# A decoder block on one core: attention's output projection as three fp32r passes instead of one f32 pass

## The reference, cut to what matters

```
qh, kh, vh = split_heads(x @ Wq), split_heads(context @ Wk), split_heads(context @ Wv)   # 8 x 2048 x 128 each
sim  = einsum('hid,hjd->hij', qh, kh) * 128 ** -0.5
mean = sim.mean(-1);  sim = (sim - mean) * 1.5 + mean
attn = softmax(sim)
out  = einsum('hij,hjd->hid', attn, vh)            # per head 2048 x 128
x    = x + merge_heads(out) @ Wout + bout          # the output projection: per head 128 x 256 of Wout
```

## Time and profile before

| | us |
|---|---|
| median of 3 runs | 1335.17 |
| lowest and highest of them | 1331.78, 1336.15 |
| the profiled execution, device time | 1332.3 |
| its span in the profile | 1330.2 |
| PE busy | 1287.7 (97%) |
| DVE, ACT, POOL busy | 1023.5 (77%), 895.9 (67%), 907.9 (68%) |
| TensorE clock granted, mean | 0.99 |

### The profile page before, as it was taken

How to read it: one execution, slowest core, us unless ns; L and a number is a source line. 1 busy time by engine, 2 the same in 40 slices (tenths; PEclk the granted TensorE clock), 3 DMA queues, 4 the chain that set the end, 5 groups by cost and what they waited for, 6 DMA issues and landing times. The chain is left out here.

```text
span 1330.2 us, 22729 instructions
## 1 busy us (share of the span) xinstructions
PE 1287.7 (97%) x8358; PEld 1077.1 (81%) x8358; DVE 1023.5 (77%) x1628; ACT 895.9 (67%) x1315; POOL 907.9 (68%) x645
## 2 busy tenths in 40 slices
PE   5999999999999999999999999999999999988998
PEld 4688888888887788888888888888888888777998
DVE  6355498759317889999999999999999899985554
ACT  4555433425655878878778778778787777775774
POOL 2544410225410899989989999999999989863553
PEclk9999999999999999999999999999999999997999
DMA  6703032246764989988888888888888888796672
GB/s 219 104 6 74 4 101 81 67 130 245 208 233 140 247 213 231 221 196 216 215 203 215 216 201 218 215 196 221 214 201 217 201 191 208 185 252 244 203 230 76
DMA packets 172377, 241.35 MB, mean 181 GB/s; under 512 B 34179, under 2 KB 78085, under 8 KB 172272
## 3 DMA queue, kind: packets, MB, share of 16 engines
q1 hardware_dynamic: 155040, 208.11, 62.0%
q10 hardware_dynamic: 15184, 25.96, 5.7%
q0 software_dynamic: 2048, 5.90, 1.1%
HBM read 64.79 MB, written 41.32 MB: 80 GB/s over the span
## 5 line engine op out<-in xcount | busy, mean ns | idle before, releaser
L1217 POOL TENSOR_TENSOR xa_pT<-xa_moved,xa_pT 128x1024 fp32r<-128x1024 f32 x246 | 589.0, 2428 | 27.1 <-ACT xa_pT L1735 26.0
L1557 PE MATMUL xa_S<-xa_kT,xa_qT 128*128 128x512 f32 x1536 | 389.1, 401 | 1.2 <-ACT xa_probs L1741 1.2
L1741 ACT ACTIVATE xa_probs<-xa_S,xa_mx_nb_rinv 128x1024 f32<-128x1024 f32 x256 | 285.9, 1117 | 146.8 <-DVE xa_mx_nb_rinv L1339 146.8
L1574 PE MATMUL xa_O<-xa_pT,xa_v 128*128 128x512 f32 x1536 | 377.2, 394 | 2.9 <-DVE xa_pT L1392 2.6
L1336 DVE TENSOR_REDUCE xa_mx_nb_rinv<-xa_S 128x1 f32<-128x1024 f32 x256 | 305.3, 1211 | 78.1 <-PE xa_S L1557 78.0
L1574 PEld LDWEIGHTS xa_O<-xa_pT,xa_v 128*128 128x128 f32 x1536 | 289.0, 189 | 69.9 <-DVE xa_pT L1392 2.9
L1557 PEld LDWEIGHTS xa_S<-xa_kT,xa_qT 128*128 128x128 f32 x1536 | 288.5, 188 | 67.9 <-ACT xa_probs L1741 2.9
L1349 DVE STREAM_TRANSPOSE xa_tq<-xa_probs 128x1024 f32<-128x1024 f32 x256 | 316.7, 1238 | 15.0 <-ACT xa_probs L1741 7.3
L1735 ACT ACTIVATE xa_pT<-xa_moved 128x1024 fp32r<-128x1024 f32 x254 | 253.9, 1050 | 2.1 <-PE xa_O L1574 1.1
L506 PE MATMUL fw_pp<-fw_hT,fw_wqk 128*128 128x512 f32 x384 | 95.0, 405 | 4.3 <-DVE fw_hT L647 4.3
L506 PEld LDWEIGHTS fw_pp<-fw_hT,fw_wqk 128*128 128x128 f32 x384 | 73.4, 194 | 20.7 <-DVE fw_hT L647 3.0
(11 more groups left out here) (247 smaller groups left out, 1679.1 us busy)
## 6 DMA issues: line engine op xcount, KB each, us to landing
xa_moved<-xa_tq SPq DMA_DIRECT2D x508, 256.0 KB, 4.5
heads_k<-ci_outs SPq DMA_DIRECT2D x32, 256.0 KB, 2.0
heads_v<-ci_outs SPq DMA_DIRECT2D x32, 256.0 KB, 2.3
heads_q<-ci_outs SPq DMA_DIRECT2D x32, 256.0 KB, 2.4
xa_chunk<-heads_v ACTq DMA_DIRECT2D x32, 256.0 KB, 4.2
ex_w1s<-in_L_ffn_w_dram SPq DMA_DIRECT2D x8, 1024.0 KB, 7.3
ex_w2s<-in_L_ffn_w_dram SPq DMA_DIRECT2D x8, 1024.0 KB, 9.7
xa_chunk<-heads_q ACTq DMA_DIRECT2D x31, 256.0 KB, 4.2
```

The source lines that it names most:

```text
L1217: pool.tensor_tensor(quadrants(pT[LO], r), unit_moved(r), quadrants(pT[HI], r).bitcast(F32), ALU.subtract).then_inc(lo_ready, 1)
L1557: last = pe.matmul(banks[:, k % 2], qT[a][:, i // GT % 2, q], kT[b][h % 2][:, k * 512:(k + 1) * 512], start=(n == 0), stop=(n == 2))
L1574: last = pe.matmul(O[:], v[a][:, j * P:(j + 1) * P], pT[b][:, r % PRING, k], start=(j == 0 and n == 0), stop=(j == JT - 1 and n == 2))
L1741: act.activation(probs[:, unit % RING], S[:, score_banks(unit)].rearrange("p a b -> p (a b)"), ACT.Exp, bias=nb[:, s % 2:s % 2 + 1], scale ...
```

## The change

- For groups 0 to 27 (heads 0 to 6, `SPLIT_GROUPS = 28`) ACT copies the bank `O` into `oTs[HI]` as fp32r, at the end of slot 4g+10 and not at the start of slot 4g+11, and DVE subtracts it from `O` into `oTs[LO]` (`output_low`, first on DVE in slot 4g+11). The bank is free for `weighted` when that is done: PE waits for `out_lo`.
- The head of Wout is split too, as a thirteenth chunk ("w", h, 0) of each head from 0 to 6 in the table: HI part on ACT, LO part on POOL, 128 x 256.
- A projection of two tiles is then 6 fp32r matmuls (3 parts for each tile) in place of 2 float32 ones (4 instructions). Head 7 stays as it was.
- Projections and additions of groups 0 to 27 come one slot later (4g+12, 4g+14 and 4g+13, 4g+15).
- The ring `chunk` is gone: its place holds `oTs[HI]` and the two parts of Wout. A chunk lands in the buffer of its own LO part (`raw_k`, `raw_v`, `raw_q`), ACT writes its HI part, and POOL subtracts in place. The load is issued at the end of the slot before the one in which it is split, and takes over the waits for the old contents from `chunk_high`.
- The table of chunks is new: k, q, v and w in slots 0, 1, 3 to 8 and 10 to 14 of a head. SP loads `woh` at the start of each head, once the "w" chunk of the head before is split.

```diff
+        raw_k = [home(f"xa_rawk{i}", f"kT{i}", [P, TOK], F32, LO * 4 * TOK) for i in range(2)]
...
+        wohs = [home(f"xa_wouts{a}", "chunk", [P, D], F32R, 4 * (GCOLS + D * a)) for a in (HI, LO)]
...
+        oTs = [home("xa_oT_hi", "chunk", [P, GCOLS], F32R),
+               nc.alloc_sbuf_tensor_at("xa_oT_lo", [P, GCOLS], F32R, offset=oT_at)]
...
+        SPLIT_GROUPS = SLOTS // GT - 4
...
         def output_slot(g, k):
-            return SLOTS + OUTPUTS[g, k] if (g, k) in OUTPUTS else (g + 1) * GT + LAG + 2 * k
+            return SLOTS + OUTPUTS[g, k] if (g, k) in OUTPUTS else (g + 1) * GT + LAG + 2 * k + (g < SPLIT_GROUPS)
         def sum_slot(g, k):
-            return SLOTS + SUMS[g, k] if (g, k) in SUMS else (g + 1) * GT + LAG + 1 + 2 * k
+            return SLOTS + SUMS[g, k] if (g, k) in SUMS else (g + 1) * GT + LAG + 1 + 2 * k + (g < SPLIT_GROUPS)
+        def group_of_outputs(s):
+            g, phase = divmod(s - LAG - GT, GT)
+            return g if phase == 0 and 0 <= g < SPLIT_GROUPS else None
...
-            plan = {0: ("k", h + 1, 0), 1: ("q", h, 1), 2: ("k", h + 1, 1), 3: ("k", h + 1, 2), 4: ("v", h, 0),
...
+            plan = {0: ("k", h + 1, 0), 1: ("q", h, 1), 3: ("k", h + 1, 1), 4: ("q", h, 2), 5: ("v", h, 0), 6: ("v", h, 1),
...
+            def output_low(g):
+                dve.wait_ge(oT_ready, g + 1)
+                if g:
+                    dve.wait_ge(y_mm, 2 * g)
+                dve.tensor_tensor(by_tile(oTs[LO][:]), by_quadrant(O[:]), by_tile(oTs[HI][:]).bitcast(F32),
+                                  ALU.subtract).then_inc(out_lo, 1)
...
             for s in range(END):
+                g = group_of_outputs(s)
+                if g is not None:
+                    output_low(g)
                 if s < SLOTS:
                     maxima(s)
...
-                if q == 0 and g:
+                if q == 0 and 0 < g <= SPLIT_GROUPS:
+                    pe.wait_ge(out_lo, g)
+                elif q == 0 and g:
                     pe.wait_ge(oT_ready, g)
...
-                    last = pe.matmul(output_bank(g, k)[:, m], oT[:, t * P:(t + 1) * P], woh[:], start=True, stop=True)
+                    if g < SPLIT_GROUPS:
+                        for n, (a, b) in enumerate(PARTS):
+                            last = pe.matmul(output_bank(g, k)[:, m], oTs[a][:, t], wohs[b][:], start=(n == 0), stop=(n == 2))
...
-                if GT <= p <= SLOTS and p % GT == 0:
+                if GT <= p <= SLOTS and p % GT == 0 and group_of_outputs(s) is None:
                     copy_oT(p // GT - 1)
...
+                if group_of_outputs(s + 1) is not None:
+                    copy_oT(group_of_outputs(s + 1))
                 if s < SLOTS:
                     for c in chunks_of(s):
                         chunk_high(c)
+                    for c in chunks_of(s + 1) if s + 1 < SLOTS else ():
+                        if c[0] != "w":
+                            load(place[c])
```

More of the change, by code:

```diff
@@ L904, in cross_block @@
         first_in = [sem(f"xa_first_in{i}") for i in range(FIRST)]
-        chunk_in = [sem(f"xa_chunk_in{i}") for i in range(CRING)]
+        chunk_in = sem("xa_chunk_in")
         chunk_hi, chunk_lo = sem("xa_chunk_hi"), sem("xa_chunk_lo")
@@ L1063, in staged @@
                 return moved[:].rearrange("p r q j n -> p (r q j n)")[:, n * UNIT:(n + 1) * UNIT]
-            return chunk[:, n % CRING]
+            kind, h, part = order[n]
+            cols = slice(part * UNIT, (part + 1) * UNIT)
+            if kind == "k":
+                return raw_k[h % 2][:, cols]
+            if kind == "w":
+                return woh[:]
+            return raw_v[:, cols] if kind == "v" else raw_q[:, part % 2]
         def target(c, a):
@@ L1147, in _ @@
                 h, i = divmod(p, TILES)
[L1148 to L1149 removed]
+                if h and i == 0:
+                    sp.wait_ge(chunk_lo, place["w", h - 1, 0] + 1)
                     sp.dma_start(woh[:], w_out[h * XD:(h + 1) * XD, :]).then_inc(wo_in, 16)
@@ L1205, in chunk_low @@
                 n = place[c]
-                kind, h, part = c
-                if kind == "v" and h == 0:
-                    for u in range(UNITS - OUTS, UNITS):
-                        if u % OUTS == part + 1:
-                            written(pool, u)
                 pool.wait_ge(chunk_hi, n + 1)
@@ L1578, in out_project @@
             def out_project(g, k):
-                if k == 0:
+                if k == 0 and g < SPLIT_GROUPS:
+                    pe.wait_ge(chunk_lo, place["w", g // 4, 0] + 1)
+                    pe.wait_ge(out_lo, g + 1)
+                elif k == 0:
                     pe.wait_ge(oT_ready, g + 1)
@@ L1588, in out_project @@
                 for m in range(2):
-                    t = 2 * k + m
-                    last = pe.matmul(output_bank(g, k)[:, m], oT[:, t * P:(t + 1) * P], woh[:], start=True, stop=True)
+                    t = slice((2 * k + m) * P, (2 * k + m + 1) * P)
+                    if g < SPLIT_GROUPS:
+                        for n, (a, b) in enumerate(PARTS):
+                            last = pe.matmul(output_bank(g, k)[:, m], oTs[a][:, t], wohs[b][:], start=(n == 0), stop=(n == 2))
+                    else:
+                        last = pe.matmul(output_bank(g, k)[:, m], oT[:, t], woh[:], start=True, stop=True)
                 last.then_inc(y_mm, 1)
@@ L1785, in _ @@
                 copy_out(n)
-            for n in range(FIRST, FIRST + CRING):
-                load(n)
             act.wait_ge(w_lo, 2)
```

75 lines of the change are left out of this document (43 added, 32 removed).

## The result

The change makes the kernel faster: 1326.61 us (median of 7 runs, 1322.67 to 1331.61) against 1333.3 for the kernel before beside it (7 runs, 1330.49 to 1339.75). The ratio is 0.9949, with 95% between 0.9926 and 0.9971. The profiled execution took 1325.07 us, where the one before had 1332.3. The gain is 0.5%, small, but the interval excludes no change.

What follows compares the result with a forecast made beforehand. PE was taken as the bound, busy for all 95.52 us of a head. Terms -7.5 (passes) and +1.2 (new wait) gave -6.3, from the four-execution mean 1333.9 to 1327.6, forecast as 1327.5 us, range 1322 to 1338.

Steps and rivals of the forecast that it cites:

- The sum: Whole run: -7.5 + 1.2 = -6.3 us, giving 1327.5 us from the mean of four executions of the kernel before.
- The passes: PE's projections: six fp32r matmuls take 0.72 us instead of 0.86, gaining 0.14 each, 7.8 us over 56.
- rival 4: PE's projections: passes cost only 0.106 us each, gaining 12.3 before deductions, time 1323 us; chance 0.06.
- Where the gain does not arrive at once: Head 0: POOL's pace keeps the first two projections from gaining, -0.3 of the 7.8 us, leaving -7.5.
- the one on the loads: Chunk and Wout loads: issued early enough, with ACT's time to spare, to cost nothing; 1 us allowed for the range.
- The new wait at (28, 0): Slot 123: PE waits once, 1.2 us, until DVE has added (27, 1), as both halves use bank Y.
- The hand-over: Bank O between groups, 28 times: costs nothing, with 0.3 us left, a margin existing only since the projections moved.
- DVE and POOL: Per head: DVE gains 2.8 us of subtractions, 4.5 idle stay; POOL needs 91.7 against 94.4; neither costs anything.
- Rival 3: POOL becomes the bound in slots with a full chunk, losing 6.7 us of gain, time 1334 us; chance 0.05.
- a maximum's delay: DVE's maxima start half a microsecond later behind the subtraction; priced at nothing, without cover up to 0.5 per group.
- Rival 2: POOL holds up DVE's subtraction, PE waits 0.5 us in 27 groups, 1341 us; chance 0.12, including similar-sized engine waits.

Runs made afterwards that it cites:

- Experiment 9: Changed kernel with SP's stores of head 0's units UNITS - 4 and UNITS - 3 put ahead of moves(1): 1326.0 us in one run.
- Experiment 10: Changed kernel with the output addition (27, 1) put ahead of the maxima in DVE's order of slot 123: 1328.41 us in one run.
- experiment 6: Changed kernel with three 128x1 memsets on DVE in front of each subtraction: 1324.76 us, ratio 0.9946 to the kernel before.
- Experiment 7: Changed kernel with projections and additions back in the old slots and "w" split at tile 9: 1333.33 us, ratio 1.0014 to the kernel before.
- experiment 2: Changed kernel with the third pass (LO, HI) of each split projection left out: 1315.33 us, ratio 0.9876 to the kernel before.
- experiment 4: Changed kernel with DVE's subtraction reading the copied HI part twice, both inputs in SBUF: 1353.13 us, ratio 1.0142 to the kernel before.

## Why the prediction was right, point by point

**The sum.** Forecast 1327.5, measured 1326.6 in the median; the profiled execution changed by -7.2, of which slots 0 to 127 have -6.3.

**The passes.** Forecast 0.14 per projection (0.86 to 0.72), measured 0.167 (0.88 to 0.71). The mechanism held, both ends were off by 0.01 to 0.02: I had put a plain slot at 5.54 where it is 5.53, twice in one subtraction, and the two small errors added up on the same side. In 53 projections that is 8.8 us; for the 54 behind my -7.5 it would be -9.0. The passes cost 0.12 each, as the experts' rows said; 0.106 (rival 4) is out. The Trainium skill (FP8 and Floating Point Precision, TensorE Precision Notes) has true FP32 as four passes. By passes alone, three against four, the projection would have gone to 0.66, a gain of 0.22, which is an estimate; the traces do not agree. The gain is 0.17, since with four passes for each of the two tiles a float32 pass cost 0.88 / 8 = 0.110 us here, and an fp32r pass 0.71 / 6 = 0.118.

**Where the gain does not arrive at once.** I gave 0.3 us to POOL's pace in head 0, and slots 7 to 17 got slower by 2.5. The step that failed is the one on the loads: "Nothing, with 1 us for the range". I had looked at when a load lands and at the time ACT has to spare. The section on the change says that the load takes over the waits for the old contents from `chunk_high`; for v of head 0 most of them come from POOL's `chunk_low`, and my working gave none of them a price. On ACT such a wait stands in front of two exponentials. Experiment 9 moves the store ahead, and 2.1 of the 2.5 come back.

**The new wait at (28, 0).** Forecast 1.2 us, once; measured 1.22 on PE and 1.4 in the stretch. Experiment 10 shows its cause.

**The hand-over.** Forecast 0.3 us of margin; it is 0.32, and at least 0.26 by experiment 6. The sentence that the margin exists only since the projections moved was half of it. Experiment 7 shows the size, 8.8 us in slots 17 to 123, and its timeline shows the other half: the addition that the move takes out of slot 4g+10. The section on the change names it behind the order of DVE, but my working gave it no price.

**DVE and POOL.** POOL 92.0 per 94.4 us (forecast 91.7 per head) and DVE 89.4, both short of PE. Rival 3 was wrong: in experiment 2 PE still sets the pace with heads of 92.26 us, 1.9 shorter than here. That a maximum's delay costs nothing held, too.

**Rival 2** was wrong for the reason given, one input in PSUM: experiment 4 makes it true by the other operand, at 1353 us, where I had reckoned 1341. I had not foreseen single holds of 7 to 9 us, and two of them make three quarters of the loss.

**What I did not see at all** is the end of the three old waits for Wout, -1.45 us. I had costed the moved load as safe and never asked whether it had been late before.

So the forecast's -6.3 for attention, which came to the tenth, is partly luck: three of the terms behind it were off by 1.4 to 2.6 us and cancelled, and the wait in head 0 alone differs by more than 1 us between executions. The passes gave 1.4 more in slots 17 to 123 than I had reckoned (8.8 against 53 x 0.14 = 7.4) and Wout another 1.45; head 0 cost 2.6 more, and slots 123 to 127 0.2 more.

## What to carry to other kernels

When a load gets a new destination, ask what is still in that memory and who waits for it to be free, and what stands on the issuing queue behind that wait. The same wait cost nothing on one engine and 2 us on another. An engine with a fifth of its time to spare can still hold up the critical one by a single DMA that waits. When a term is the difference of two nearly equal distances in a trace, take both from starts of rows and carry the hundredths, because 56 repetitions turned 0.027 us into 1.5. And a step that gains on the critical engine may be worth all of its gain or none, by whether another piece of work is in the same slot: list for the slots around a hand-over everything that each engine does there, before and after.

## What the runs showed of the hardware

- A DVE operation on 128x512 with both inputs in SBUF (experiment 4) took 691 ns at best, 1216 in the median and 8757 at worst beside a busy POOL; with one input in PSUM, 691 to 693 in all 28. I knew of the median's kind, not that one operation can be held through several of POOL's, as 2 of the 28 were.
- Six fp32r matmuls of 256 columns take 0.71 us where four float32 instructions of that size took 0.88.
- Memsets of 128x1 on DVE cost little: 59 ns each, and three of them delayed what stands behind them by 0.26 us in all (experiment 6).
- A DMA issue that waits on ACT holds the activations behind it: 2.37 us of waiting on an ACT that is busy for 68% of the span left PE idle for 1.33 us (slot 7 of the changed kernel).
